# New places for every step of a two-stage language tower: same instructions, another order on each engine

## The reference, cut to what matters

```
h = tower(x)        # x: 32 x 256 token ids; embedding 128 wide, 2 layers, 8 heads
                    # per layer: layer norm, q/k/v, causal filter over k and v, gates from v and k,
                    # gated causal linear attention, each head divided by its norm, output product,
                    # layer norm, gelu network 128 -> 512 -> 128; at the end layer norm, head 128 -> 256
h = h + attention(layernorm(h))    # 16 heads of 64: q (k'v) / 8, then W_o; no softmax
h = h + ffn(layernorm(h))          # 256 -> 768 -> 256, silu(gate) * up, int weights / 127
```

## Time and profile before

| what | value |
|---|---|
| time, median of 3 runs | 1989.66 us (1988.47 to 1992.6) |
| the profiled execution | 1988.27 us, span 1986.1 us |
| PE busy | 1850.2 us, 93% |
| DVE busy | 1165.6 us, 59% |
| ACT, POOL busy | 733.4 us, 439.4 us |
| stage A with all streams full | about 60 to 820 us, one group each 50.9 us |
| hand-over | about 820 to 950 us |
| stage B | about 950 to 1986 us, one group each 66.2 us |

### The profile page before, as it was taken

How to read it: one execution, slowest core, us unless ns; L and a number is a source line. 1 busy time by engine, 2 the same in 40 slices (tenths; PEclk the granted TensorE clock), 3 DMA queues, 4 the chain that set the end, 5 groups by cost and what they waited for, 6 DMA issues and landing times.

```text
span 1986.1 us, 41766 instructions
## 1 busy us (share of the span) xinstructions
PE 1850.2 (93%) x17146; PEld 1588.0 (80%) x17146; DVE 1165.6 (59%) x3019; ACT 733.4 (37%) x1444; POOL 439.4 (22%) x391
## 2 busy tenths in 40 slices
PE   4799999999999999969899999999999999999998
PEld 3678888888888888758688888888888888888887
DVE  2668888888888888755554344434444444444443
ACT  1334444554455555334323322232233223322332
POOL 3233223333222222111121122112211221122112
PEclk8899999999999999989899999999999999999999
DMA  3000000000000000022000000000000000000000
GB/s 94 5 12 18 18 17 18 16 19 16 18 17 16 15 5 9 18 86 80 17 22 1 22 22 22 1 22 22 22 1 22 22 22 1 22 22 22 1 22 22
DMA packets 29211, 42.38 MB, mean 21 GB/s; under 512 B 5856, under 2 KB 22624, under 8 KB 29024
## 3 DMA queue, kind: packets, MB, share of 16 engines
q1 hardware_dynamic: 23648, 33.49, 5.1%
q0 software_dynamic: 2048, 4.20, 0.8%
q10 hardware_dynamic: 3328, 2.04, 0.4%
HBM read 22.93 MB, written 16.78 MB: 20 GB/s over the span
## 4 chain that ended last, share of the span: by engine, by line
PE 73%; DVE 17%; issue 4%; DMA 3%; POOL 2%; ACT 1%; SPq 1%; another core or an unknown queue 0%; DVEq 0%; POOLq 0%; ACTq 0%
PE ps L1406 11%; PE ps L1407 10%; PE ps L1408 10%; PE ps L806 3%; PE ps L1008 3%; PE ps L1456 3%; PE ps L1472 3%; DVE bxn L1271 3%; PE ps L887 3%; PE ps L807 3%; PE ps L808 3%; PE ps L959 3%; PE ps L937 2%; DVE bstats L1255 2%; DMA h<-h_rows 2%
## 5 line engine op out<-in xcount | busy, mean ns | idle before, releaser
L1245 POOL TENSOR_TENSOR hids_low<-hid,hids_high 128x512 fp32r<-128x512 f32 x96 | 137.6, 1440 | 611.0 <-ACT hids_high L1392 611.0
L512 POOL TENSOR_TENSOR rstd<-var,minus_half 128x4 f32<-128x4 f32 x80 | 82.5, 1032 | 564.5 <-DVE var L599 564.4
L757 ACT ACTIVATE xn<-x,shift,rstd 128x128 f32<-128x128 f32 x320 | 130.3, 482 | 133.6 <-DVE shift L604 133.6
L676 DVE TENSOR_TENSOR att<-ps,causal 128x512 f32<-128x512 f32 x256 | 158.6, 681 | 18.1 <-PE ps L937 18.0
L1406 PE MATMUL ps<-r_high,wq_high 128*128 128x256 f32 x512 | 147.4, 288 | 0.7 <-issue 0.7
L1407 PE MATMUL ps<-r_low,wq_high 128*128 128x256 f32 x512 | 144.9, 283 | 0.0
L1408 PE MATMUL ps<-r_high,wq_low 128*128 128x256 f32 x512 | 144.8, 283 | 0.0
L1386 ACT ACTIVATE silu<-ps 128x512 f32<-128x512 f32 x96 | 57.4, 598 | 226.5 <-DVE hid L1321 159.9
L1008 PE MATMUL ps<-w_f,wide 128*128 128x128 f32 x1024 | 130.1, 278 | 0.2 <-ACT wide L801 0.2
L1008 PEld LDWEIGHTS ps<-w_f,wide 128*128 128x128 f32 x1024 | 120.8, 192 | 6.0 <-issue 5.0
L1308 DVE TENSOR_TENSOR m_low<-ps,m_high 128x512 fp32r<-128x512 f32 x32 | 22.1, 692 | 170.8 <-ACT m_high L1378 170.8
(11 more groups left out here) (352 smaller groups left out, 5060.9 us busy)
## 6 DMA issues: line engine op xcount, KB each, us to landing
h_rows<-h_out SPq DMA_DIRECT2D x16, 512.0 KB, 2.8
h<-h_rows SPq DMA_DIRECT2D x16, 512.0 KB, 3.8
out<-bxn SPq DMA_DIRECT2D x32, 256.0 KB, 2.6
taps<-in_filters ACTq DMA_DIRECT2D x1, 1024.0 KB
emb<-in_embed,idx POOLq DMA_INDIRECT x64
wk<-in_W_kT SPq DMA_DIRECT2D x1, 1024.0 KB, 6.6
stage<-in_W_vT SPq DMA_DIRECT2D x2, 512.0 KB, 6.6
stage<-in_W_q SPq DMA_DIRECT2D x2, 512.0 KB, 5.6
```

The costliest lines, as they stand in the source:

```text
L512: pool.tensor_tensor(rstd[s][:], var[s][:], minus_half[:], ALU.pow)\
L676: dve.tensor_tensor(masked[:, :, PAIR * g:PAIR * g + PAIR, :], bank("qk", s, l, j, g, t)[:].rearrange("p (n r t) -> p n r t", n=2, r=PAIR) ...
L757: act.activation(xn[s][:, j, :], x[s][:, j, :], ACT.Identity, bias=shift[s][:, j:j + 1], scale=rstd[s][:, j:j + 1]).then_inc(xn_made[s].se ...
L1245: pool.tensor_tensor(hids[1][:, halves, :], hid[:, half, :], hids[0][:, halves, :].bitcast(F32), ALU.subtract).then_inc(hid_low[s].sem, 1)
```

## The change

Every number of the five tables is replaced. No function, instruction, buffer or wait is changed; nothing is added or taken away. Only the order on each engine changes, and with it the PSUM banks. The lines of the diff with the steps that the prediction speaks of:

```diff
@@ PLACES_A
...
-            ("conv_out", 0, 1, 1151), ("turn_v", 0, 0, 944), ("vT_out", 0, 0, 1309), ("gate", 0, 0, 1233),
-            ("gate_mul", 0, 0, 1176), ("gated", 0, 0, 1450), ("state", 0, 0, 1415), ("state_low", 0, 0, 1494),
...
-            ("chain", 0, 0, 1714), ("unit", 0, 0, 1687), ("unit_out", 0, 0, 1814), ("wo", 0, 0, 1835),
-            ("wo_out", 0, 0, 1875), ("stats", 1, 0, 1875), ("pow", 1, 0, 2227), ("shift", 1, 0, 1929),
-            ("xn", 1, 0, 1961), ("turn", 1, 0, 1922), ("high", 1, 0, 2209), ("low", 1, 0, 1969),
...
-            ("turn", 4, 0, 3921), ("high", 4, 0, 3996), ("low", 4, 0, 3977), ("head", 0, 0, 3977),
-            ("head_out", 0, 0, 3981), ("head", 0, 1, 3998), ("head_out", 0, 1, 3999), ("idx", 0, 0, 145),
-            ("gather", 0, 0, 1320), ("gather", 0, 1, 2415), ("gather", 0, 2, 2784), ("gather", 0, 3, 3374),
...
+            ("conv_out", 0, 1, 1308), ("turn_v", 0, 0, 979), ("vT_out", 0, 0, 1593), ("gate", 0, 0, 1207),
+            ("gate_mul", 0, 0, 1210), ("gated", 0, 0, 1441), ("state", 0, 0, 1654), ("state_low", 0, 0, 1524),
...
+            ("chain", 0, 0, 1795), ("unit", 0, 0, 1794), ("unit_out", 0, 0, 1894), ("wo", 0, 0, 1915),
+            ("wo_out", 0, 0, 1941), ("stats", 1, 0, 1945), ("pow", 1, 0, 2247), ("shift", 1, 0, 1960),
+            ("xn", 1, 0, 2217), ("turn", 1, 0, 1965), ("high", 1, 0, 2489), ("low", 1, 0, 1975),
...
+            ("turn", 4, 0, 3964), ("high", 4, 0, 3999), ("low", 4, 0, 3982), ("head", 0, 0, 3984),
+            ("head_out", 0, 0, 3983), ("head", 0, 1, 3998), ("head_out", 0, 1, 3999), ("idx", 0, 0, 1364),
+            ("gather", 0, 0, 2870), ("gather", 0, 1, 3213), ("gather", 0, 2, 3622), ("gather", 0, 3, 3739),
...
@@ STARTS_B
-STARTS_B = [18529, 19796, 21058, 22323, 23587, 24851, 26115, 27378, 28634, 29890, 31147, 32409, 33658, 34916, 36173,
-            37440]
+STARTS_B = [18511, 19761, 21015, 22270, 23519, 24771, 26022, 27273, 28527, 29782, 31036, 32285, 33538, 34789, 36039,
+            37294]
@@ PREPARE
...
-PREPARE = [("w_load", 0, 18419), ("w_high", 0, 18243), ("w_low", 0, 18125), ("w_load", 1, 18430),
-           ("w_high", 1, 19037), ("w_low", 1, 18986), ("w_load", 2, 18565), ("w_high", 2, 19290),
...
+PREPARE = [("w_load", 0, 15655), ("w_high", 0, 18193), ("w_low", 0, 17988), ("w_load", 1, 17331),
+           ("w_high", 1, 18218), ("w_low", 1, 18033), ("w_load", 2, 17741), ("w_high", 2, 19110),
...
```

More of the change, by code:

```diff
@@ L69 @@
[L69 to L73, removed]
-            ("gram_high", 1, 0, 986), ("gram_low", 1, 0, 941), ("t1", 0, 0, 794), ("t1_even", 0, 0, 987),
-            ("t1_odd", 0, 0, 959), ("t1", 0, 1, 823), ("t1_even", 0, 1, 996), ("t1_odd", 0, 1, 972),
-            ("keys", 0, 0, 843), ("keys_out", 0, 0, 1016), ("keys", 0, 1, 875), ("keys_out", 0, 1, 1036),
-            ("r", 0, 0, 972), ("r_high", 0, 0, 1055), ("r_low", 0, 0, 993), ("r", 0, 1, 1041),
-            ("r_high", 0, 1, 1104), ("r_low", 0, 1, 1060), ("m", 0, 0, 1048), ("m", 0, 1, 1056), ("m", 0, 2, 1062),
-            ("m_high", 0, 0, 1133), ("m_low", 0, 0, 1094), ("attn", 0, 0, 1113), ("attn_out", 0, 0, 1139),
-            ("t1", 1, 0, 964), ("t1_even", 1, 0, 1044), ("t1_odd", 1, 0, 991), ("t1", 1, 1, 1012),
-            ("t1_even", 1, 1, 1083), ("t1_odd", 1, 1, 1017), ("keys", 1, 0, 1042), ("keys_out", 1, 0, 1117),
-            ("keys", 1, 1, 1043), ("keys_out", 1, 1, 1121), ("r", 1, 0, 1063), ("r_high", 1, 0, 1141),
-            ("r_low", 1, 0, 1097), ("r", 1, 1, 1071), ("r_high", 1, 1, 1160), ("r_low", 1, 1, 1098),
-            ("m", 1, 0, 1096), ("m", 1, 1, 1103), ("m", 1, 2, 1112), ("m_high", 1, 0, 1206), ("m_low", 1, 0, 1123),
-            ("attn", 1, 0, 1143), ("attn_out", 1, 0, 1144), ("b_stats", 1, 0, 1161), ("b_pow", 1, 0, 1082),
-            ("b_xn", 1, 0, 1201), ("b_turn", 1, 0, 1207), ("b_high", 1, 0, 1321), ("b_low", 1, 0, 1204),
-            ("b_turn", 1, 1, 1210), ("b_high", 1, 1, 1384), ("b_low", 1, 1, 1218), ("b_gate", 0, 0, 1341),
-            ("b_up", 0, 0, 1569), ("silu", 0, 0, 1409), ("hid", 0, 0, 1470), ("hid_high", 0, 0, 1593),
-            ("hid_low", 0, 0, 2009), ("b_gate", 1, 0, 1393), ("b_up", 1, 0, 1657), ("silu", 1, 0, 1471),
-            ("hid", 1, 0, 1807), ("hid_high", 1, 0, 1924), ("hid_low", 1, 0, 2025), ("b_gate", 2, 0, 1552),
-            ("b_up", 2, 0, 1679), ("silu", 2, 0, 1501), ("hid", 2, 0, 2048), ("hid_high", 2, 0, 2429),
-            ("hid_low", 2, 0, 2196), ("b_gate", 3, 0, 1592), ("b_up", 3, 0, 1958), ("silu", 3, 0, 1700),
-            ("hid", 3, 0, 2106), ("hid_high", 3, 0, 2490), ("hid_low", 3, 0, 2300), ("b_gate", 4, 0, 1683),
-            ("b_up", 4, 0, 2430), ("silu", 4, 0, 1961), ("hid", 4, 0, 2433), ("hid_high", 4, 0, 2493),
-            ("hid_low", 4, 0, 2404), ("b_gate", 5, 0, 1944), ("b_up", 5, 0, 2437), ("silu", 5, 0, 2236),
-            ("hid", 5, 0, 2437), ("hid_high", 5, 0, 2495), ("hid_low", 5, 0, 2473), ("down", 0, 0, 2340),
-            ("down", 1, 0, 2387), ("down", 2, 0, 2440), ("down", 3, 0, 2444), ("down", 4, 0, 2490),
-            ("down", 5, 0, 2494), ("add", 0, 0, 2489), ("add", 1, 0, 2497), ("send", 0, 0, 2466)]
```

110 lines of the change are left out of this document (70 added, 40 removed).

## The result

The changed kernel takes 2019.3 us (2016.24 to 2022.38, 4 runs) against 1989.07 for the kernel before, run beside it: 1.0148 times as long, 95% interval 1.013 to 1.0165. I had forecast 1987, 1970 to 1998. The profiled execution took 2020.52 us, its span is 2018.4.

What follows compares the result with a forecast made beforehand. PE, busy 93% of the span and waiting mostly for DVE, was taken to bound the kernel. 1988.3 - 8.8 (stage A) + 9.8 (stage B) - 0.5 (start-up) - 2.2 (hand-over) = 1986.6, taken as 1987 us, range 1970 to 1998.

Steps and rivals of the forecast that it cites:

- Stage A, gains: Stage A: embed leaves gated 0 and bias 0 leaves state_low 1 on POOL, so PE waits less; -2.6 us per group.
- the sum of stage A: Stage A: gains, two new waits and two small terms together, -0.6 us per group, bounds -1.9 and +0.7.
- New wait one: Stage A: turn 1 on PE waits for conv_out 0, behind xn 1 and high 4 on ACT; +0.9 us per group.
- rival two: ACT becomes what PE waits for, stage A gains nothing and stage B pays; 1995.4 us or 2000, chance 0.23.
- New wait two: Stage A: bias 0 on POOL runs inside chain 0 on DVE, which ends 1.25 us later; +0.7 us per group.
- Stage B: All stage B terms together: +0.65 us per group, +9.8 us over 15 groups.
- rival one: Stage B: POOL doesn't get in between the b_xn instructions, only hid_low 3 holds them up; 1969 us, chance 0.24.
- the changes of kind: Stage B, PE: each stretch of split products after fp32 steps costs 0.2 us extra; +0.25 us per group.
- the two `attn`: Stage B, PE: down 1 no longer stands between the attns, so attn 0 covers twelve narrow matmuls; +0.1 us per group.
- `hid 5`: Stage B: hid 5 now stands behind b_xn, so down 5 starts later; +0.3 us per group.
- Start-up: Start-up: two waits go, about -1.7 us, while bias 0 meets chain 0, +1.2; together -0.5 us.
- the hand-over: Hand-over: the 1.4 us wait for rows_low goes and b_load meets fewer transfers; -2.2 us, between -6 and +3.

Runs made afterwards that it cites:

- with 16 columns: The changed kernel with each bias step on POOL adding only 16 of 512 columns, order and waits untouched; ratio 0.986 to the kernel before.
- the widths: The changed kernel with each bias step cut to 16, 256 or 384 of 512 columns; ratios 0.986, 1.0021 and 1.0117 to the kernel before.
- the fourth version: The kernel before with POOL's stage A order laid by hand and embed behind pow 3 and one gather; ratio 1.0068 to the kernel before.

## Why the prediction was wrong

The step that failed is "Stage A, gains": it took the POOL steps away from where they met small DVE instructions and put nothing but a `gather` in their place. So the sum of stage A, -0.6 us per group, has no term for the new meetings, and a group took 2.3 us more.

- *That embed leaves gated 0 and bias 0 leaves state_low 1* was right: L650 is at 0.69, the wait for `gk` went from 10.1 to 0.4 us. The size, -2.6, is not refuted: with 16 columns, where the biases hold hardly anything but the wait for `kc` is still there (6.9 us in 10 groups), a group went from 50.9 to 49.3, -1.6; my terms without the one of `bias 0` on `chain 0` give -1.3. (14 groups at -0.6 are -8.4, not the -8.8 written.)
- *What stands in their place* is the mistake. I wrote "in its place stands a gather" and followed POOL no further. Behind that gather stands `bias 1`, and on DVE behind `gated 0` stands `shift 3`, 0.15 us long and on SBUF. `shift 3` then pushes `mask .1` and `xn 3` back by 1.6, and `embed` and `bias 3` come to lie on `state_low 0`: L664, which was to be at 0.19 throughout, takes 1.28 in 11 of 24 cases. `bias 2` comes to lie on `shift 4` (1.24 us). I had moved each meeting away from where it was and had not drawn the new POOL timeline over all small DVE instructions. That POOL's order alone costs 24.8 of 29.8 us, and the widths, show that it is these meetings. Only `bias 1` on `shift 3` was taken away by itself (53.2 -> 51.8); how the rest divides among the others was not measured.
- *The granted clock* has no term in the prediction. It falls in about every second group of stage A, behind a starved `turn 3` and a wait of 1.47 us, but costs little here: 53.2 us with the fall, 53.0 without, because it takes a wait of 1.1 away.
- *New wait one* (+0.9): it is there, 0.7 printed, once per group. Taken away beside the other holds it gave nothing (51.8 and 51.8 us), since PE then waits for `state_low`. My rival two had this mechanism as the cause of a slower result; its sign came true, its cause did not.
- *New wait two* (+0.7): there. `chain 0` is held in nearly every group, by 1.9 us at L694 in the four groups at full clock, where PE waits 1.1 for `sq`, and by 0.7 to 1.1 at L688 in the others, where it waits 0.3 once. I had said 1.25 throughout.
- *Stage B*, forecast +0.65 per group, measured 7.5/15 = 0.5: right in size, and in part by luck, since inside it two terms are off in opposite ways. Both `hid_low 3` and `hid_low 4` get in between the `b_xn` instructions, as the forecast had it and rival one had not:

```profile
1243.06 3.31 DVE L1271 TENSOR_SCALAR bxn<-h,bmv,brstd 128x256 f32<-128x256 f32 x4 [0.47 <-POOL brstd L1235]
...
1244.35 1.38 DVE L1271 TENSOR_SCALAR bxn<-h,bmv,brstd 128x256 f32<-128x256 f32 x1
```

```profile
1242.99 2.58 POOL L1245 TENSOR_TENSOR hids_low<-hid,hids_high 128x512 fp32r<-128x512 f32 x2
```

  But a held `b_xn` hides its own 0.4 us in the hold, so the four take 3.31 us, not 3.9, and PE waits 0.3 where it waited 0.85: -0.5 instead of 0. Against that the changes of kind cost up to 6.9/15 = 0.46 instead of 0.25, and the two `attn` side by side take 3.10 us where they took 1.44 each, 0.2 for 0.1. For `hid 5` (0.3) the run gives 0.2, no more than the scatter. These four terms sum to 0.4 of the 0.5.
- *Start-up* gave 5.7 us instead of 0.5, the hand-over cost 0.8 instead of giving 2.2. The two together are 2.2 better than recorded. I did not look into them.

The bounds of stage A were summed from the waits I had listed; none held a new meeting that I had not seen, so the range ended at 1998.

## What to carry to other kernels

When an order changes on an engine whose instructions hold up another's, lay the whole new timeline of both engines side by side and look at every short instruction, not at the ones that were held before; keep the holding instructions under work that reads PSUM. When TensorE's granted clock falls behind such waits, the time moves from the idle into the busy column. What the fall costs is read by comparing whole groups with and without it: here 0.3 us in one kernel, and 3.5 in another, where it took no wait away. Places that come from a search with a model of durations want a gap wider than the model's error, else neighbouring groups get different orders.

## What the runs showed of the hardware that I had not expected

The hold starts before POOL's recorded start. L694 of the fourth version (417.93) begins 0.63 us ahead of the bias (418.56), with 0.19 us of work, and is still held, while L690 at 417.73 is not; `shift 3` (501.32) begins 0.40 ahead of its bias (501.72). In both a gather is still running on POOL. The gather alone holds nothing (L650 of the changed kernel, 500.70 for 0.69 under the gather of 500.67), and with a bias of 16 columns behind it neither: there shift 3 starts at 518.24, 0.41 ahead of the bias, and takes 0.17. So behind a gather, meetings read from recorded starts come out too few by some 0.4 to 0.7 us before a wide POOL instruction (0.73 for the L694 of 299.99, whose bias is recorded at 300.72); why a narrow one does not do it stays open. The hold can also pass from one bias to the next without letting DVE in, 3.19 us over two of them, where one `b_xn` instruction got in between two `hid_low`.

The Trainium skill, "SBUF — State Buffer", section "SBUF: two separate sides", has the lock last for the whole instruction. The widths agree: `shift 3` takes 1.2, 1.4 and 1.72 us beside a bias of 0.73, 1.00 and 1.27. That whoever starts first gets it does not agree with the recorded starts behind a gather, by which DVE was first.
